# The calls of four engines in the first stage of an RWKV and mixture-of-experts kernel, in another order

## The reference

```python
x = _layernorm(x + rwkv_block(x))
x = _layernorm(x + moe_block(x))

# rwkv_block
x = _ln(x, ln0_w, ln0_b); h = _ln(x, ln1_w, ln1_b); xx = time_shift(h)
k = (h * tmk + xx * (1 - tmk)) @ Wk.T        # v, r in the same way
att = wkv(-exp(time_decay), time_first, k, v)  # recurrence over the 256 tokens, by channel
x = x + (sigmoid(r) * att) @ Wo.T
h2 = _ln(x, ln2_w, ln2_b); xx2 = time_shift(h2)
kv = square(relu(mix(h2, xx2, cmk) @ Wfk.T)) @ Wfv.T
x = x + sigmoid(mix(h2, xx2, cmr) @ Wfr.T) * kv

# moe_block, 12 experts, top 2
ys = geglu(x @ Ws1 + bs1) @ Ws2 + bs2            # shared expert
w  = softmax over the 2 highest of (x @ Wr + br) / 1.5
yr = sum over those 2 of w_e * (geglu(x @ We1[e] + be1[e]) @ We2[e] + be2[e])
```

## Time and profile before

| | |
|---|---|
| median of 3 runs | 462.53 us (461.55 to 463.85) |
| profiled execution | 463.21 us |
| its span, first to last instruction | 461.4 us |
| mean granted TensorE clock | 0.953 |
| busy: PE, DVE, ACT, POOL | 390.9, 310.2, 293.0, 246.7 us |
| first expert matmul after the head | 268.9 us |
| end of the experts' steady stretch | about 429.9 us |

### The profile page before, as it was taken

One profiled execution on the slowest core, in us unless ns is written; L12 is line 12 of the kernel. 1 busy time (PEld: TensorE's weight loads), 2 busy tenths in 40 slices (PEclk: granted clock), 3 DMA queues, 4 the chain that ended last, 5 costly groups with the idle time before them and its releaser, 6 DMA issues.

```text
span 461.4 us, 9878 instructions
## 1 busy us (share of the span) xinstructions
PE 390.9 (85%) x2487; PEld 302.6 (66%) x2487; DVE 310.2 (67%) x1097; ACT 293.0 (64%) x723; POOL 246.7 (53%) x300
## 2 busy tenths in 40 slices
PE   0757799998988888976799499999999999999690
PEld 0224466757746565654344179999999999999530
DVE  6979988999996995741372266666666656665183
ACT  4478799989796955633121067777777766777062
POOL 4756855648388867777347114444444444444252
PEclk9978799999999999997899599999999999999997
DMA  8699100000003101011262137777776776762483
GB/s 230 151 288 348 46 0 1 1 1 1 2 18 104 32 13 44 30 50 42 82 203 83 54 136 248 259 244 261 247 254 243 258 250 238 253 239 104 132 328 106
DMA packets 47248, 64.86 MB, mean 141 GB/s; under 512 B 8797, under 2 KB 31069, under 8 KB 47193
## 3 DMA queue, kind: packets, MB, share of 16 engines
q1 hardware_dynamic: 42584, 54.50, 34.9%
q0 software_dynamic: 4448, 9.38, 6.1%
q10 hardware_dynamic: 160, 0.35, 0.3%
HBM read 21.65 MB, written 13.91 MB: 77 GB/s over the span
## 4 chain that ended last, share of the span: by engine, by line
PE 55%; DVE 14%; ACT 9%; another core or an unknown queue 8%; issue 5%; POOL 4%; DMA 2%; POOLq 0%; SPq 0%; DVEq 0%; ACTq 0%
PE bank L1396 22%; PE bank L1414 11%; DVE bst L487 3%; PE bank L1042 3%; ACT z L725 2%; PE bank L1060 2%; PE bank L1441 2%; PE bank L1108 2%; PE bank L1388 2%; DVE rec L576 1%; PE bank L1091 1%; DMA we_sb<-routed_rows 1%; PE bank L983 1%; PE bank L1071 1%
## 5 line engine op out<-in xcount | busy, mean ns | idle before, releaser
L1235 POOL DMA_INDIRECT routed_rows<-yo,goes_to x75 | 71.8, 957 | 103.8 <-DVE yo L1288 101.4
L1396 PE MATMUL bank<-xT,w 128*128 128x128 f32 x896 | 112.9, 275 | 0.0
L1396 PEld LDWEIGHTS bank<-xT,w 128*128 128x128 f32 x896 | 106.4, 192 | 0.8 <-issue 0.5
L1280 DVE SCALAR_TENSOR_TENSOR actT<-bank,tile_bias,gl 128x128 f32<-128x128 f32 x225 | 65.4, 346 | 24.8 <-ACT gl L1348 13.5
L413 POOL DMA_INDIRECT dispatched_rows<-rows_all,slot_i x64 | 64.3, 1005 | 30.1 <-issue 17.7
L1348 ACT ACTIVATE gl<-bank,tile_bias 128x128 f32<-128x128 f32 x225 | 66.2, 363 | 15.2 <-PE bank L1396 7.9
L1414 PE MATMUL bank<-we_sb,actT 128*128 x450 | 62.8, 276 | 1.0 <-DVE yo L1288 0.9
L1414 PEld LDWEIGHTS bank<-we_sb,actT 128*128 128x128 f32 x450 | 56.1, 192 | 1.5 <-issue 1.5
L1288 DVE SCALAR_TENSOR_TENSOR yo<-bank,goes,wb 128x128 f32<-128x128 f32 x75 | 26.3, 351 | 36.7 <-PE bank L1414 33.0
L1342 ACT ACTIVATE xT<-bank 128x128 f32<-128x128 f32 x74 | 20.5, 277 | 25.2 <-PE bank L1388 24.9
L1042 PE MATMUL bank<-xk,wfk_sb 128*128 128x512 f32 x64 | 33.0, 625 | 3.4 <-DVE xk L593 1.8
(11 more groups left out here) (220 smaller groups left out, 764.6 us busy)
## 6 DMA issues: line engine op xcount, KB each, us to landing
w<-we_sb SPq DMA_DIRECT2D x75, 384.0 KB
x_all<-dispatched_rows SPq DMA_DIRECT2D x75, 68.0 KB
we_sb<-we SPq DMA_DIRECT2D x1, 4608.0 KB
we_sb<-routed_rows SPq DMA_DIRECT2D x8, 512.0 KB, 7.4
rows_all<-x SPq DMA_DIRECT2D x8, 256.0 KB, 5.1
out<-x_all SPq DMA_DIRECT2D x8, 256.0 KB, 2.3
routed_rows<-yo,goes_to POOLq DMA_INDIRECT x75
dispatched_rows<-rows_all,slot_i POOLq DMA_INDIRECT x64
```

What stands on the lines that cost most here:

```text
L1235: ng.indirect_dma_start(routed, bass.IndirectOffsetOnAxis(ap=goes_to[n // U % DB][:, n % U:n % U + 1], axis=0), yo[n % YO][:, :], None).th ...
L1280: nv.scalar_tensor_tensor(actT[n % UA][:, at], ps_a[j][:, 0:P], tile_bias[:, j, n:n + 1], gl[n % 2][:, at], ALU.add, ALU.mult).then_inc(s2 ...
L1396: return nt.matmul(to[:, 0:P], w1[m][:, off:off + P], xT[m][:, :], start=True, stop=True)
```

## The change

The four lists of calls are written in another order. The same calls with the same arguments stand in them, except that GpSimd's 64 scatters are cut into fewer pieces (0 to 7, 7 to 9, 9 to 16, 16 to 23, 23 to 29 and 29 to 64, where it had eleven). No function is changed. The later parts of the four lists, which hold what the prediction speaks of; the lists before them differ in the same manner.

```diff
@@ -687,26 +687,27 @@
...
-            placed(v, 0, pT[:, PT_PREFIX]); one_over(5); output(5); weigh_v(6); stats2(5)
-            states(6); maximum(7); carried(6); gaps(7); x3(4); mix(5); stats3(4); one_over(6); output(6)
-            logits(3); chosen(v, 1); stats2(6); weigh_v(7); logits(4); states(7); carried(7); x3(5); stats3(5)
-            mix(6); placed(v, 1, pT[:, PT_PREFIX]); one_over(7); output(7); shared_act(0, 0); logits(5)
-            stats2(7); chosen(v, 2); shared_act(0, 1); x3(6); mix(7); stats3(6)
-            shared_act(1, 0); placed(v, 2, pT[:, PT_PREFIX]); find_tiles(0); leave_tiles(); x3(7); shared_act(1, 1); stats3(7)
-            shared_take(0); logits(6); shared_act(2, 0); shared_act(2, 1); tell_tiles(0); logits(7); chosen(v, 3)
-            shared_take(1); shared_act(3, 0); shared_act(3, 1); placed(v, 3, pT[:, PT_PREFIX])
...
...
+            x3(2); logits(1); stats3(2); weigh_v(5); stats2(4); states(5); chosen(v, 0); carried(5); maximum(6)
+            gaps(6); one_over(5); output(5); x3(3); stats3(3); mix(4); logits(2); stats2(5); weigh_v(6)
+            states(6); carried(6); placed(v, 0, pT[:, PT_PREFIX]); maximum(7); gaps(7); one_over(6); output(6)
+            weigh_v(7); x3(4); mix(5); stats3(4); states(7); shared_act(0, 0); logits(3); carried(7); stats2(6)
+            one_over(7); output(7); shared_act(0, 1); chosen(v, 1); mix(6); logits(4); x3(5); stats3(5)
+            stats2(7); placed(v, 1, pT[:, PT_PREFIX]); shared_act(1, 0); logits(5); chosen(v, 2); mix(7)
+            shared_take(0); shared_act(1, 1); x3(6); stats3(6); placed(v, 2, pT[:, PT_PREFIX]); find_tiles(0)
+            x3(7); stats3(7); shared_act(2, 0); shared_take(1); shared_act(2, 1); logits(6); shared_act(3, 0)
+            shared_act(3, 1); leave_tiles(); tell_tiles(0); logits(7); chosen(v, 3); shared_take(2)
...
@@ -836,32 +837,32 @@
...
-            relu(5, 0); square(5, 0); relu(5, 1); norm3(4); relu(5, 2); relu(5, 3); square(5, 1); x1(6)
-            by_channel(4); square(5, 2); square(5, 3); gate2(5); fallen(a, 1); norm2(6); affine2(6); affine2k(6)
-            shared_gelu(0, 0); gate(7); norm3(5); shared_gelu(0, 1); relu(6, 0); relu(6, 1); by_channel(5)
-            square(6, 0); relu(6, 2); square(6, 1); relu(6, 3); x1(7); square(6, 2); square(6, 3); norm2(7)
-            gate2(6); affine2(7); affine2k(7); shared_gelu(1, 0); fallen(a, 2); relu(7, 0); square(7, 0)
-            relu(7, 1); square(7, 1); relu(7, 2); square(7, 2); relu(7, 3); square(7, 3); norm3(6)
-            shared_gelu(1, 1); gate2(7); by_channel(6); shared_gelu(2, 0); shared_gelu(2, 1)
-            norm3(7); by_channel(7); shared_gelu(3, 0); shared_gelu(3, 1); fallen(a, 3)
-            shared_gelu(4, 0); shared_gelu(4, 1); place_pad(7); shared_gelu(5, 0); place_pad(8)
-            shared_gelu(5, 1); place_pad(9); shared_gelu(6, 0); place_pad(10); shared_gelu(6, 1); place_pad(11)
-            shared_gelu(7, 0); first_take(0); shared_gelu(7, 1)
...
+            relu(4, 0); by_channel(3); relu(4, 1); gate(6); affine1(7); norm2(5); relu(4, 2); relu(4, 3)
+            square(4, 2); square(4, 0); square(4, 1); square(4, 3); affine2(5); below(7); factors(7)
+            affine2k(5); gate2(5); shared_gelu(0, 0); relu(5, 0); square(5, 0); relu(5, 1); x1(6); square(5, 1)
+            norm3(4); relu(5, 2); square(5, 2); relu(5, 3); square(5, 3); shared_gelu(0, 1); gate(7); norm2(6)
+            by_channel(4); affine2(6); affine2k(6); gate2(6); relu(6, 0); square(6, 0); relu(6, 1); x1(7)
+            square(6, 1); fallen(a, 1); shared_gelu(1, 0); norm3(5); relu(6, 2); relu(6, 3); by_channel(5)
+            norm2(7); shared_gelu(1, 1); square(6, 2); square(6, 3); affine2k(7); fallen(a, 2); affine2(7)
+            relu(7, 0); square(7, 0); relu(7, 1); relu(7, 2); relu(7, 3); square(7, 1); square(7, 2)
+            square(7, 3); norm3(6); shared_gelu(2, 0); gate2(7); shared_gelu(2, 1); shared_gelu(3, 0); norm3(7)
+            by_channel(6); shared_gelu(3, 1); by_channel(7); shared_gelu(4, 0); fallen(a, 3); shared_gelu(4, 1)
+            shared_gelu(5, 0); shared_gelu(5, 1); shared_gelu(6, 0); place_pad(7); shared_gelu(6, 1)
+            place_pad(8); place_pad(9); shared_gelu(7, 0); shared_gelu(7, 1); place_pad(10); place_pad(11)
+            first_take(0)
@@ -940,20 +941,17 @@
...
-            weigh0(6); shift0(6); deviation(3, "2"); add_new(4); weigh0(7); deviation(6, "1")
-            shift0(7); deviation(2, "3"); deviation(7, "1"); residual(3); deviation(4, "2"); add_new(5)
-            residual(4); deviation(3, "3"); scatter_rows(g, 0, 7); deviation(5, "2"); scatter_rows(g, 7, 9)
-            add_new(6); scatter_rows(g, 9, 11); deviation(4, "3"); scatter_rows(g, 11, 13); residual(5)
-            scatter_rows(g, 13, 15); deviation(6, "2"); scatter_rows(g, 15, 16); add_new(7); deviation(5, "3")
-            residual(6); scatter_rows(g, 16, 23); deviation(7, "2"); scatter_rows(g, 23, 28); residual(7)
-            scatter_rows(g, 28, 29); deviation(6, "3"); scatter_rows(g, 29, 38); deviation(7, "3")
-            scatter_rows(g, 38, SLOTS // P)
...
+            deviation(2, "3"); deviation(7, "1"); deviation(4, "2"); add_new(5); residual(4); deviation(3, "3")
+            deviation(5, "2"); add_new(6); scatter_rows(g, 0, 7); residual(5); deviation(4, "3")
+            scatter_rows(g, 7, 9); add_new(7); deviation(6, "2"); scatter_rows(g, 9, 16); residual(6)
+            deviation(5, "3"); deviation(7, "2"); scatter_rows(g, 16, 23); residual(7); deviation(6, "3")
+            scatter_rows(g, 23, 29); deviation(7, "3"); scatter_rows(g, 29, SLOTS // P)
@@ -1137,29 +1135,30 @@
...
-            hidden(5, 2); hidden(5, 3); rwkv(6); turn3(4); receptance2(5); router(4); mixed_channels(5)
-            turn2(6); receptance(7); shared_gate(0, 0); prefix(1); hidden(6, 0); hidden(6, 1); shared_gate(0, 1)
-            turn3(5); hidden(6, 2); hidden(6, 3); router(5); rwkv(7); shared_gate(1, 0); shared_up(0, 1)
-            receptance2(6); mixed_channels(6); turn2(7); shared_back(0); prefix(2); hidden(7, 0); hidden(7, 1)
-            shared_up(1, 0); hidden(7, 2); hidden(7, 3); shared_gate(1, 1); receptance2(7); mixed_channels(7)
-            shared_up(1, 1); turn3(6); shared_gate(2, 0); router(6); shared_gate(2, 1); shared_up(2, 0); tell(0)
-            shared_gate(3, 0); shared_back(1); turn3(7); shared_up(2, 1); router(7); shared_up(3, 0)
-            shared_gate(3, 1); shared_back(2); shared_up(3, 1); prefix(3); shared_gate(4, 0); shared_back(3)
-            shared_up(4, 0); shared_gate(4, 1); shared_up(4, 1); shared_gate(5, 0); shared_back(4)
...
...
+            values(7); mixed_channels(4); receptance2(5); rwkv(6); shared_gate(0, 0); router(3); hidden(5, 0)
+            hidden(5, 1); shared_up(0, 0); hidden(5, 2); hidden(5, 3); shared_gate(0, 1); shared_up(0, 1)
+            turn3(4); receptance(7); mixed_channels(5); turn2(6); rwkv(7); receptance2(6); router(4)
+            hidden(6, 0); hidden(6, 1); shared_gate(1, 0); hidden(6, 2); prefix(1); shared_back(0); hidden(6, 3)
+            turn3(5); shared_up(1, 0); shared_gate(1, 1); router(5); shared_up(1, 1); turn2(7)
+            shared_gate(2, 0); mixed_channels(6); hidden(7, 0); hidden(7, 1); shared_up(2, 0); hidden(7, 2)
+            hidden(7, 3); prefix(2); receptance2(7); mixed_channels(7); shared_back(1); shared_gate(2, 1)
+            shared_gate(3, 0); shared_up(2, 1); shared_up(3, 0); turn3(6); shared_back(2); shared_up(3, 1)
+            shared_gate(3, 1); router(6); tell(0); turn3(7); shared_gate(4, 0); router(7); shared_back(3)
+            shared_gate(4, 1); shared_gate(5, 0); shared_up(4, 0); shared_up(4, 1); prefix(3); shared_up(5, 0)
+            shared_back(4); shared_gate(5, 1); shared_up(5, 1); shared_gate(6, 0); shared_up(6, 0)
...
```

More of the change, by code:

```diff
@@ L694, in attention_vector @@
-            x3(0); stats3(0); mix(1); one_over(2); output(2); stats1(5); weigh_v(3)
-            stats2(2); states(3); maximum(4); carried(3); gaps(4); x3(1); mix(2); stats3(1); one_over(3)
-            logits(0); output(3); weigh_v(4); states(4); stats2(3); carried(4); maximum(5); stats1(6); gaps(5)
-            one_over(4); x3(2); mix(3); stats3(2); logits(1); stats1(7); output(4); chosen(v, 0); weigh_v(5)
-            stats2(4); states(5); logits(2); maximum(6); carried(5); gaps(6); x3(3); mix(4); stats3(3)
@@ new lines, in attention_vector @@
+            one_over(3); maximum(4); gaps(4); output(3); x3(1); stats3(1); logits(0); mix(2); weigh_v(4)
+            stats2(3); states(4); carried(4); stats1(7); one_over(4); maximum(5); gaps(5); output(4); mix(3)
+            x3(2); logits(1); stats3(2); weigh_v(5); stats2(4); states(5); chosen(v, 0); carried(5); maximum(6)
+            gaps(6); one_over(5); output(5); x3(3); stats3(3); mix(4); logits(2); stats2(5); weigh_v(6)
+            states(6); carried(6); placed(v, 0, pT[:, PT_PREFIX]); maximum(7); gaps(7); one_over(6); output(6)
@@ L843, in attention_scalar @@
```

(23 more changed lines are left out.)

63 lines of the change are left out of this document (31 added, 32 removed).

## The result

| | kernel before | changed kernel |
|---|---|---|
| median beside each other | 463.19 us (461.55 to 464.13, 4 runs) | 467.93 us (465.99 to 472.04, 4 runs) |
| profiled execution, its span | 463.21, 461.4 us | 468.41, 466.7 us |
| first expert tile | 268.9 us | 273.6 us |

The ratio is 1.013, 95% interval 1.0085 to 1.018: 1.3% slower, where 456.5 us was forecast.

A forecast was written before the change was run, and what follows sets the result against it. Bound by VectorE to 178 us, by late hand-offs to 268.9, then by a full TensorE. 1 us gained up to `placed(3)` and 5 after make 6: 462.5 - 6 = 456.5 us, range 449 to 468, likeliest case 451 to 460.

The forecast's parts named there:

- The bound: 178 to 268.9 us: hand-off chain, four unnamed pieces of 34.8 us together, guessed to be TensorE results held by scatter runs.
- Step 1: Recurrence up to `output(7)`: 7.4 us less VectorE work ahead, new waits +2.5, so 5 us earlier, between 1 and 11.
- Step 2: From `output(7)` to `stats3(7)`: ends about 4 us earlier than 208.9, near 205; `norm3(7)` can run by about 209.
- Step 3: From `stats3(7)` to `placed(3)`: 235 us, near before; 222 with nothing held, about 240 with everything held.
- second rival: Run of 19 scatters holds `turn3(7)` to its end: `placed(3)` 240, first tile 273, 466.5 us in all; chance 0.32.
- Step 4: From `placed(3)` to the first tile: 33 us before, about 5 us gained, at least 0, at most 15.
- The clock: Before the first tile: granted clock 0.81 and 0.84, half level after TensorE idles; cost stays, inside the 33 us.
- first rival: Nothing held in the new order: `placed(3)` at 222, first tile 245 to 250, 438 to 444 us; chance 0.12.

The follow-up runs named there:

- p6: Changed kernel with one pause of three idle GpSimd operations after scatter 34: 468.2 us beside 463.5 for the kernel before, ratio 1.014.
- p7: Changed kernel with two idle GpSimd operations after every fourth scatter from number 19 on: 461.3 us beside 463.5 for the kernel before, ratio 0.995.
- a1: Changed kernel, unaltered, on a chip where the kernel before took 438.8 us: 432.5 us, ratio 0.985.

## Why the prediction was wrong

**The bound.** That the loss sits in four unnamed pieces within GpSimd's runs was read rightly, and the guess on their cause is borne out by p6 and p7. What they cost was not known: on a quiet chip the kernel before takes 24 us less, all of it ahead of the first tile. By that their 34.8 us in the chain are worth 24 us, since TensorE's own work is the next bound.

**Step 1, `output(7)` 5 us earlier (between 1 and 11).** Too small: 13 us on the chip of the prediction (177.02 to 163.81), 12 on a quiet one. Two terms were mis-sized. Up to its end VectorE is busy 124.7 us from 30 us on instead of 134.2, 9.5 us less where I had counted 7.4. And the waits went down by 3.7 us (13.5 to 9.8) where I had them rise by 2.5: the waits of the old order that the new one removes were seen, but given less weight than the new ones at `weigh_v`.

**Step 2, `stats3(7)` ended near 205, `norm3(7)` near 209.** 206.4 and 208.94. Near enough, by luck: step 1 gave 8 us more than forecast, and of the 13 us gained at `output(7)` only 2.5 are left here; the unnamed pieces at 169.34 and 198.13 take 8.9 between (before, the one at 179.02 took 4.2). In a1, where nothing is held, `stats3(7)` ends at 198.2.

**Step 3, `placed(3)` near 235.** This is the step that failed: 244.5. The argument for 235 was that the old run "has nearly the same length and held each of these steps too". It did hold `turn3(7)`, but the same length isn't the same end. Before, scatters 29 to 37 went out from 198.26 us on, while `stats3(7)` was still to come, then came `deviation(7, "3")` as a pause, and the run ended at 223.7. In the new order `deviation(7, "3")` stands ahead of all 19: GpSimd first waits 4.13 us for the statistics, starts the run at 208.40, and ends it at 232.15 without a pause, 8.4 us later than before. The prediction had this run from 207 to 231 in its own text and didn't use it for the 235. `turn3(7)` is done 4.6 us sooner than before and read 6.1 us later, and from its reading to `placed(3)` it takes 12.7 us where it took 9.9, since more matmuls stand between `router(7)` and `prefix(3)`, and the first of them run at the half clock (eight of `router(7)` 1.85 us and four of `shared_back` 3.76, where a1 has 1.03 and 1.96). That makes the 8.9 us. The second rival had this mechanism, and its condition, too: `turn3(7)` not through by 212 us (it was at 217.7). It put `placed(3)` at 240. What I held against that rival, that GpSimd pauses at scatter 48 in any case, was a circle: that pause comes only after number 47, and it waits for `placed(3)`, which itself waits for the held result.

**Step 4, 28 us from `placed(3)` to the first tile.** 29.1 us (244.5 to 273.6; before 33.3). Right within 1 us, but the 28 us were no fixed cost: 13.7 of the 29.1 are two unnamed pieces (254.47 and 264.65). p6 shows what that means. It puts `placed(3)` at 233.9, where the forecast had it, and the first tile still comes at 273.1, 39 us behind it. So step 3 alone put right wouldn't have given 263 either; that held results are no constant of the tail, but move with the run, was missing in both steps. And that the second rival's 273 is met to 1 us has some luck in it: `placed(3)` came 4.5 us later than it said, and the rest took 4 us less than its 33.

The sum is then: 13 us ahead of before at `output(7)`, 2.5 ahead at `stats3(7)`, 8.9 behind at `placed(3)`, 4.7 behind at the first tile.

**The clock.** From 205 to 236 us the granted clock is 0.73, against 0.81 before and 1.00 in a1: where TensorE had waited it is at the half level for a time, so a held result costs more than its own length. The Trainium skill (TensorE: Matmul & The Clock Gate, What's actually happening) has the gate follow how busy the engine was; these rows agree.

**The first rival** (nothing held, 438 to 444 us) got a chance of 0.12. On quiet chips it is what happens, and goes further: `placed(3)` at 217 and 222 in two traces, where it had 222, then 18 us to the first tile in both instead of 20 to 25, and 432.5 us. It was worked out as a question of the new order. It is one of the chip, or of the hour, and there the old order gains 24 us as well. The sign of the change hangs on this: 1.3% and 1.1% slower where results are held, 1.5% and 1.3% faster where not.

## What to carry to other kernels

A wait without a named releaser that sits in a long run of software-issued transfers is to be priced on its own before an order is judged: put pauses into the run and read when the held result comes (the total time can hide it, as in p6), and take the time again on another chip. When two orders are compared, look when each run ends, and where its pauses fall, against the results that the rest waits for; a pause that waits for the held result itself is none. And where an engine becomes the bound once the holds are gone, an earlier producer brings nothing unless that engine's own list has work in the place.
